# Two strided reduces in place of four pairwise maxima, and three projections moved to later rounds, in an attention and mixture-of-experts block on one core

## The chip, the core and the metric

The kernel runs on one NeuronCore of a Trainium2 chip. Its engines work from queues of their own and wait for each other by semaphores: PE (TensorE, matmuls), DVE (VectorE), ACT (ScalarE), POOL (GpSimd) and SP (SyncE, which starts transfers). The metric is the time of one execution on the device in microseconds (us). Times inside an execution come from one profiled execution and count from the start of its span.

## What is computed

A layer norm, then the input plus attention plus a mixture of experts. Attention has 4 sequences of 1024 tokens with 256 channels and one head; the mixture sends every token to 2 of 16 experts beside a shared network.

```python
xn = _layernorm(x, axis=-1)
x = x + attn(xn, Wq, bq, Wk, bk, Wv, bv) + ffn(xn, ...)

def attn(x, Wq, bq, Wk, bk, Wv, bv):
    q = jnp.einsum('bte,de->btd', x, Wq) + bq
    k = jnp.einsum('bte,de->btd', x, Wk) + bk
    v = jnp.einsum('bte,de->btd', x, Wv) + bv
    dot = jnp.einsum('bqd,bkd->bqk', q, k) / KSQRT
    p = jax.nn.softmax(dot, axis=-1)
    return jnp.einsum('bqk,bkd->bqd', p, v)
```

Everything is fp32. Each product is made of three matmuls of a high and a low part (`PASSES`), so every operand is split: ACT writes the high part, DVE the remainder.

## The kernel before

The function `plan` writes a list of steps. Every engine's program goes through the same list and does its own part of each step, in order; an engine never passes a step of its own. What sets the order of the work is thus this list alone, together with the semaphores on which a part waits.

The shared network and the experts come first, up to about 323 us. The rest, which the change touches, is attention. Its tokens are cut into 8 groups of 512 queries (`g`, 4 tiles of 128 each, tile numbers n = 4g to 4g + 3); sequence b has groups 2b and 2b + 1. The text calls the work of one g a round. A round has these steps:

- `scores` g, pair (0 to 3): PE makes the scores of 256 keys for 512 queries, 12 matmuls of 512 columns, into two banks of PSUM. `scores_copy`: ACT copies them to `scored_t` in SBUF (keys on partitions). `scored_t` is overwritten by pair 0 of the next round, so ACT waits there until the last `less` of the round before has read it.
- `scores_max`: DVE takes the maximum over the 8 key tiles for each query, elementwise, in `top_keys` (lines L1480, L1483, L1486).
- `tops`: PE turns `top_keys` (line L729, "top_keys"); `tops_max`: DVE finds each query's maximum `nmax` and spreads it to `less_wide`; `spread`: PE turns that back (L729, "less_wide").
- `less` n: DVE adds the negative maximum to the scores of tile n, giving `probs_f` (L1512, 3 buffers). `probs` n: ACT takes the exponential and copies the high part to `pT`. `probs_lo` n: DVE writes the remainder of `pT` (L1204).
- `weigh` n: PE multiplies `pT` of tile n with the values (24 matmuls, 258 columns). `weigh_sum` n: DVE divides by the sum and adds to the result `acc` (L1535, L1538), SP stores it. These four steps run in the round after, for the tiles `old` = 4(g - 1) to `old` + 3.
- `rows_in` i: DVE adds the two gathered expert rows of tile i to `acc` (L1528, twice per tile); POOL gathers the next ones (`gather`).
- projections: `heads` b, u (12 matmuls of 512 columns) makes the half u of the queries of sequence b (needed by round 2b + u) and `values` b, u (24 matmuls of 256 columns) half of its values (needed by the weighing of its tiles). ACT and DVE split the result (`heads_split`, into `qT`, L1461; `values_split`, into `vv`, L1204). These are the steps that can be moved: before the change `ahead` and `behind` name, for each round, what stands ahead of its first weigh and behind its `tops_max`.

`scores`, `heads` and `values` share two pairs of PSUM banks in turn (the "ring" in `Places`): each takes the pair that the one before the last has left, and waits until ACT and DVE have emptied it.

The lines of `scores_max` and of PE's wait for them, before:

Of the kernel before, what the change touches and what calls it, by code (L numbers as in the profile page):

```python
# [86 lines left out]
def plan():  # L87
# [119 lines left out]
    def weigh(n):  # L207
        return [("weigh", n), ("weigh_sum", n)]
# [4 lines left out]
    def probs(n):  # L213
        return [("probs", n), ("probs_lo", n)]


    ahead = {1: split("heads", 1, 1), 2: split("heads", 2, 0), 3: split("heads", 2, 1), 4: split("heads", 3, 0),
             5: split("heads", 3, 1), 6: split("values", 3, 1)}
    behind = {2: split("values", 1, 1), 3: split("values", 2, 0), 4: split("values", 2, 1), 5: split("values", 3, 0)}
    steps += [("keys_load", 1), ("ones",), *split("heads", 0, 0), *split("values", 0, 0)]  # L220
    steps += [("gather", i) for i in range(YR)]
    for g in range(GROUPS):
        new, old = CT * g, CT * (g - 1)
        steps += scores(g, 0)
        if g == 1:
            steps += probs(new - 2)
# [7 lines left out]
        if g == 0:  # L234
            steps += [*split("heads", 0, 1), ("heads", 1, 0), ("tops", g), ("tops_max", g), ("heads_split", 1, 0),
                      ("values", 0, 1), ("spread", g), ("values", 1, 0), ("less", new),
                      ("values_split", 0, 1), ("less", new + 1), ("less", new + 2), ("probs", new), ("values_split", 1, 0), ("probs", new + 1),
                      ("probs_lo", new), ("less", new + 3), ("probs_lo", new + 1), *rows(new + 2), *rows(new + 3)]
        elif g + 1 < GROUPS:
            steps += [*ahead[g], *weigh(old), ("tops", g), ("tops_max", g), *behind.get(g, []), *weigh(old + 1), ("spread", g),  # L240
                      ("less", new), ("less", new + 1), ("less", new + 2), ("probs", new), ("probs", new + 1),
                      ("probs", new + 2), ("probs_lo", new), ("less", new + 3), *weigh(old + 2), ("probs_lo", new + 1),
                      *rows(new + 2), ("probs_lo", new + 2), *rows(new + 3)]
            if g + 2 < GROUPS:
                steps += [*weigh(old + 3), *probs(new + 3)]
        else:
            steps += [("probs", new - 1), *weigh(old - 1), *weigh(old), ("tops", g), ("probs_lo", new - 1), ("tops_max", g),
                      *weigh(old + 1), ("spread", g), ("less", new), ("less", new + 1), ("less", new + 2),
                      *[("probs", new + t) for t in range(CT)], ("probs_lo", new), ("less", new + 3), *weigh(old + 2),
                      ("probs_lo", new + 1), *weigh(old + 3), ("probs_lo", new + 2), ("probs_lo", new + 3),  # L250
                      *rows(new + 2), *rows(new + 3), *sum((weigh(new + t) for t in range(CT)), [])]
# [59 lines left out]
def build(nc, x, bv, Wqkv, bqk_in, Wr, We, Ws, const_f, const_b, out):  # L311
# [4 lines left out]
    with ctx:  # L316
# [82 lines left out]
        scored_t = at("scored_t", r_h, [P, KT, CHUNK])  # L399
# [802 lines left out]
        def vector_program(e):  # L1202
# [369 lines left out]
```

## Time and profile before

| | us |
|---|---|
| median of 3 runs | 562.47 |
| lowest and highest | 562.42, 563.23 |
| the profiled execution | 562.47 |
| its span | 560.7 |
| PE busy in it | 520.9 |
| DVE busy | 396.4 |
| ACT busy | 280.4 |
| POOL busy | 191.4 |

The span is the time between the first and the last instruction; the execution's time has 1.8 us around it. Busy is the time in which an engine works on an instruction. In the timelines a row gives the start in us, the duration in us, engine, line, operation, written and read tiles, a count, and in brackets how long the engine sat idle before it and which instruction ended the wait. Where a row holds several instructions, its duration goes from the first start to the last end. Matmuls overlap: the next starts before one has ended, so their prices are read from start to start. The granted clock of TensorE has a mean of 0.991.

### The profile page before, as it was taken

How to read it: one execution, taken by the hardware profiler on the slowest of the kernel's cores; microseconds unless marked ns; L12 is line 12 of the kernel's file. 1: busy time of each engine (PE TensorE's matmuls, PEld its weight loads, DVE VectorE, ACT ScalarE, POOL GpSimd, SP SyncE). 2: the span in 40 equal slices, each digit the busy share in tenths (PEclk: the TensorE clock that was granted, in tenths of full speed). 3: DMA queues.
4: the chain of work that ended last, by engine and by line, in shares of the span. 5: the costliest groups of instructions: out<-in, count | busy, mean ns of one | idle time of the engine just before them, and what ended most of it. 6: DMA issues, size and time to landing. Idle time of an engine off the chain costs nothing.

```text
span 560.7 us, 9991 instructions
## 1 busy us (share of the span) xinstructions
PE 520.9 (93%) x3469; PEld 473.2 (84%) x3469; DVE 396.4 (71%) x806; ACT 280.4 (50%) x467; POOL 191.4 (34%) x170
## 2 busy tenths in 40 slices
PE   3999998899997899989886999999999999999997
PEld 3888987778887789988876988798989898989897
DVE  5778456998985456454453627899696969697986
ACT  3767764355643255444342544836272727272742
POOL 0001010411005666788885043244142323323410
PEclk9999999999998899999998999999999999999999
DMA  8826254302023455674447471062116111112111
GB/s 314 338 104 243 114 226 179 113 30 85 0 85 95 140 167 161 196 255 146 150 147 127 119 251 37 24 223 61 53 57 206 58 56 49 57 55 69 39 57 57
DMA packets 29888, 69.29 MB, mean 124 GB/s; under 512 B 5008, under 2 KB 9488, under 8 KB 28816
## 3 DMA queue, kind: packets, MB, share of 16 engines
q1 hardware_dynamic: 22496, 49.68, 24.7%
q0 software_dynamic: 6912, 18.88, 12.9%
q8 instruction: 30, 0.49, 0.4%
q14 instruction: 18, 0.15, 0.1%
q10 hardware_dynamic: 432, 0.09, 0.1%
HBM read 41.37 MB, written 27.26 MB: 122 GB/s over the span
## 4 chain that ended last, share of the span: by engine, by line
PE 76%; DVE 10%; another core or an unknown queue 4%; ACT 4%; issue 3%; DMA 1%; POOL 0%; SPq 0%; ACTq 0%; DVEq 0%; POOLq 0%
PE ps L723 47%; PE ps L904 8%; PE ps L729 7%; PE ps L845 6%; PE ps L925 5%; PE ps L806 1%; DVE probs_f L1512 1%; DVE blk_xT L1204 1%; ACT probs_f L1194 1%; DMA stage_gu<-in_shared 1%; ACT blk_xT L1009 1%; PE ps L815 1%; DMA blk_x<-rows,row 1%; DVE acc L1294 1%
## 5 line engine op out<-in xcount | busy, mean ns | idle before, releaser
L710 POOL DMA_INDIRECT rows_y<-ytab,slot x64 | 75.5, 1180 | 136.5 <-DVE acc L1528 120.1
L682 POOL DMA_INDIRECT blk_x<-rows,row x80 | 82.1, 1026 | 70.2 <-DVE row L1399 31.5
L723 PE MATMUL ps<-vv,pT 128*128 128x258 f32 x768 | 96.7, 284 | 0.0
L723 PE MATMUL ps<-xT,shared_w 128*128 128x512 f32 x384 | 94.3, 400 | 1.4 <-DVE sil L1280 1.4
L723 PEld LDWEIGHTS ps<-vv,pT 128*128 128x128 f32 x768 | 94.2, 189 | 0.5
L723 PEld LDWEIGHTS ps<-xT,shared_w 128*128 128x128 f32 x384 | 72.3, 192 | 16.8 <-issue 2.1
L723 PE MATMUL ps<-qT,xbT_hi 128*128 128x512 f32 x256 | 79.5, 392 | 1.0 <-ACT scored_t L1009 0.8
L904 PE MATMUL ps<-expert_w,blk_xT 128*128 x480 | 68.3, 292 | 6.6 <-DVE blk_xT L1204 6.4
L904 PEld LDWEIGHTS ps<-expert_w,blk_xT 128*128 128x128 f32 x480 | 61.1, 193 | 8.8 <-issue 8.4
L723 PEld LDWEIGHTS ps<-qT,xbT_hi 128*128 128x128 f32 x256 | 47.2, 188 | 11.9 <-ACT scored_t L1009 2.0
L668 POOL TENSOR_TENSOR expert_w<-stage_e,expert_w 128x768 fp32r<-128x768 f32 x7 | 13.6, 1941 | 115.2 <-ACT expert_w L1009 115.2
L1194 ACT ACTIVATE probs_f<-probs_f 128x1024 f32<-128x1024 f32 x32 | 33.6, 1049 | 37.7 <-DVE probs_f L1512 37.7
L723 PE MATMUL ps<-qT,xbT_lo 128*128 128x512 f32 x128 | 49.9, 390 | 0.0
L845 PE MATMUL ps<-shared_w,hT 128*128 128x256 f32 x384 | 49.6, 288 | 0.0
L1009 ACT ACTIVATE scored_t<-ps 128x1024 f32<-128x1024 f32 x32 | 32.6, 1023 | 33.0 <-PE ps L723 29.4
L845 PEld LDWEIGHTS ps<-shared_w,hT 128*128 128x128 f32 x384 | 48.1, 195 | 0.3
L1204 DVE TENSOR_TENSOR blk_xT<-ps,blk_xT 128x512 fp32r<-128x512 f32 x40 | 27.6, 689 | 25.7 <-ACT blk_xT L1009 21.0
L1132 ACT ACTIVATE blk_sil<-ps 128x256 f32<-128x256 f32 x40 | 15.4, 386 | 50.9 <-PE ps L904 24.8
L1204 DVE TENSOR_TENSOR pT<-probs_f,pT 128x1024 fp32r<-128x1024 f32 x32 | 39.0, 1219 | 2.1 <-ACT pT L1009 1.9
L925 PE MATMUL ps<-expert_w,blk_hT 128*128 x240 | 39.3, 300 | 1.1 <-DVE blk_hT L1204 1.0
L1512 DVE TENSOR_TENSOR probs_f<-scored_t,ps 128x1024 f32<-128x1024 f32 x32 | 37.6, 1215 | 1.3 <-PE ps L729 0.4
L1425 DVE TENSOR_TENSOR blk_h<-blk_sil,ps 128x256 f32<-128x256 f32 x40 | 16.7, 416 | 28.4 <-ACT blk_sil L1132 20.1
(159 smaller groups left out, 869.3 us busy)
## 6 DMA issues: line engine op xcount, KB each, us to landing
ytab<-blk_y SPq DMA_DIRECT2D x40, 256.0 KB
keys<-xT SPq DMA_DIRECT2D x8, 1024.0 KB, 5.7
stage_e<-in_experts SPq DMA_DIRECT2D x16, 384.0 KB, 3.1
rows<-xn SPq DMA_DIRECT2D x8, 512.0 KB, 2.6
xbT_hi<-keys SPq DMA_DIRECT2D x8, 512.0 KB
xbT_lo<-keys SPq DMA_DIRECT2D x8, 512.0 KB
out<-acc SPq DMA_DIRECT2D x32, 128.0 KB
acc<-in_x SPq DMA_DIRECT2D x7, 512.0 KB, 8.8
```

What stands on the lines that cost most here:

```text
L682: e.indirect_dma_start(out=blk_x[:, q, n, :], out_offset=None, in_=rows, in_offset=bass.IndirectOffsetOnAxis(ap=row[:, 2 * b + n:2 * b + n ...
L710: e.indirect_dma_start(out=rows_y[:, r, k, :], out_offset=None, in_=ytab, in_offset=bass.IndirectOffsetOnAxis(ap=slot[:, k, i:i + 1], axis=0),
L723: ins = e.matmul(dst, stationary(p, k), moving(q, k), start=(n == 0), stop=(n == total - 1))
L729: ins = e.transpose(dst[:, n * P:(n + 1) * P], s, ident)
L845: ins = e.matmul(ps[:, b, (n % 2) * D:(n % 2 + 1) * D], hT[:, p, j, n * P:(n + 1) * P], shared_w[:, q, 2 * KD * SH + j * D:2 * KD * SH + ( ...
L904: ins = e.matmul(ps[:, 2 + r, n * D:(n + 1) * D], blk_xT[:, r, p, (n * KD + k) * P:(n * KD + k + 1) * P], weights(b, n, q, k * 2 * HID, 2 ...
L925: ins = e.matmul(ps[:, 6 + r, n * D:(n + 1) * D], blk_hT[:, r, p, n * P:(n + 1) * P], weights(b, n, q, 2 * D, D), start=(at == 0), stop=(a ...
L1009: e.activation(hi, src, ACT.Copy).then_inc(done, 1)
L1194: e.activation(probs_f[w][:, :, :], probs_f[w][:, :, :], ACT.Exp).then_inc(exp_made, 1)
L1204: e.tensor_tensor(lo, src, hi.bitcast(F32), ALU.subtract).then_inc(done, 1)
L1425: e.tensor_tensor(blk_h[:, r, :, :], blk_sil[:, r, :, :], gu[:, :, HID:2 * HID], ALU.mult).then_inc(blk_hidden, 1)
L1512: e.tensor_tensor(probs_f[w][:, :, :], scored_t[:, 0:KT, t * P:(t + 1) * P], ps[:, 5, t * P:(t + 1) * P].unsqueeze(1).to_broadcast([P, KT, ...
```

## The change

It has three parts. The maximum over the 8 key tiles is made in two `tensor_reduce` on a strided view in place of three `tensor_tensor` of 1024 elements and one of 512: the first reads the first 4 tiles once the second pair of scores is copied and writes into a ninth row of `scored_t`; the second reads the last 4 tiles and that row once the fourth pair is copied. The steps ahead of and behind `tops` are made by a rule in place of the two tables, and this moves projections:

| round | projections before | after |
|---|---|---|
| 0 | heads 0.1, heads 1.0, values 0.1, values 1.0 | heads 0.1, heads 1.0, values 0.1 |
| 1 | heads 1.1 | values 1.0 |
| 2 | heads 2.0, values 1.1 | heads 1.1 |
| 3 | heads 2.1, values 2.0 | values 1.1, heads 2.0 |
| 4 | heads 3.0, values 2.1 | heads 2.1, values 2.0 |
| 5 | heads 3.1, values 3.0 | values 2.1, heads 3.0 |
| 6 | values 3.1 | heads 3.1, values 3.0, values 3.1 |

Third, `top_keys` and `less_wide` change places in SBUF, which no step waits for.

```diff
         steps += scores(g, 1)
         if g == 1:
-            steps += probs(new - 1)
-        steps += [("scores_max", g, 1), *rows(new), *scores(g, 2), ("scores_max", g, 2), *rows(new + 1)]
-        steps += [*scores(g, 3), ("scores_max", g, 3)]
-        if g in (1, 3):
-            steps.append(("keys_load", g // 2 + 2))
...
+            steps += [("probs", new - 1), ("probs_lo", new - 1)]
+        steps += [("scores_max", g, 0), *rows(new), *scores(g, 2), *rows(new + 1), *scores(g, 3), ("scores_max", g, 1)]
+        if u == 1 and b + 2 < NB:
+            steps.append(("keys_load", b + 2))
+        if first:
+            beside = [*split("heads", 0, 1), ("heads", 1, 0)], [("heads_split", 1, 0), ("values", 0, 1)], []
+            sums = [[], [], [], []]
         else:
...
+            sums = [[("weigh", old + t), ("weigh_sum", old + t)] for t in range(CT)]
+            if g == 1:
+                beside = split("values", 1, 0) + sums[0], sums[1], []
+            elif g == 2:
+                beside = split("heads", 1, 1) + sums[0], sums[1], []
+            elif u == 0:
+                beside = split("heads", b, 1) + sums[0], split("values", b, 0), sums[1]
+                if b + 1 == NB:
+                    beside[1].extend(split("values", b, 1))
+            elif not last:
+                beside = split("values", b, 1) + split("heads", b + 1, 0) + sums[0], sums[1], []
...
+        steps += [*beside[0], ("tops", g), ("tops_max", g), *beside[1], ("spread", g), *beside[2]]
+        if first:
+            steps += [("less", new), ("less", new + 1), ("less", new + 2), ("values_split", 0, 1), ("probs", new),
+                      ("probs", new + 1), ("probs_lo", new), ("less", new + 3), ("probs_lo", new + 1), *rows(new + 2), *rows(new + 3)]
...
-                    if pair == 1:
-                        if g > 0:
-                            e.wait_ge(tops_turned, g)
-                        e.tensor_tensor(top_keys[:, :, :], scored_t[:, 0:2, :], these, ALU.max).then_inc(tops_found, 1)
...
+                    g, half = a
+                    e.wait_ge(scores_copied, nth[("scores", g, 2 * half + 1)])
+                    if g > 0:
+                        e.wait_ge(tops_turned, g)
+                    if half == 1:
+                        e.wait_ge(tops_found, 2 * g + 1)
+                    these = scored_t[:, 0:KT // 2, :] if half == 0 else scored_t[:, KT // 2:KT + 1, :]
+                    e.tensor_reduce(scored_t[:, KT, :] if half == 0 else top_keys[:, :],
+                                    these.rearrange("p k q -> p q k"), X, ALU.max).then_inc(tops_found, 1)
```

What this does to the engines' queues is shown at three places. The first is DVE behind the spread turn of round 0; `qT` is the remainder of heads 1.0, `probs_f` is written by a less, the first `vv` is the remainder of values 0.1 and the second that of values 1.0. Before:

```order
L1461 SCALAR_TENSOR_TENSOR qT<-ps,mix_b,qT 128x512 x2
L1512 TENSOR_TENSOR probs_f_102<-scored_t,ps 128x1024
L1204 TENSOR_TENSOR vv<-ps,vv 128x4x256
L1512 TENSOR_TENSOR probs_f_103<-scored_t,ps 128x1024
L1512 TENSOR_TENSOR probs_f_104<-scored_t,ps 128x1024
L1204 TENSOR_TENSOR vv<-ps,vv 128x4x256
L1204 TENSOR_TENSOR pT_96<-probs_f_102,pT_96 128x1024
L1512 TENSOR_TENSOR probs_f_102<-scored_t,ps 128x1024
```

After:

```order
L1471 SCALAR_TENSOR_TENSOR qT<-ps,mix_b,qT 128x512 x2
L1516 TENSOR_TENSOR probs_f_101<-scored_t,ps 128x1024
L1516 TENSOR_TENSOR probs_f_102<-scored_t,ps 128x1024
L1516 TENSOR_TENSOR probs_f_103<-scored_t,ps 128x1024
L1214 TENSOR_TENSOR vv<-ps,vv 128x4x256
L1214 TENSOR_TENSOR pT_96<-probs_f_101,pT_96 128x1024
L1516 TENSOR_TENSOR probs_f_101<-scored_t,ps 128x1024
```

The remainder of values 0.1 went from behind one less to behind three, and that of values 1.0 is gone from here.

The second place is PE at the same point. `xbT_hi` and `xbT_lo` are the two parts of sequence 0, the names with numbers those of sequence 1; `w_v` marks a values step and `qT` scores. Before:

```order
L723 MATMUL ps<-w_v,xbT_hi 128x256 x2
L723 MATMUL ps<-w_v,xbT_lo 128x256
L729 MATMUL ps<-cf,less_wide 128x128 x4
L723 MATMUL ps<-w_v,xbT_hi_92 128x256 x2
L723 MATMUL ps<-w_v,xbT_lo_93 128x256
```

After:

```order
L733 MATMUL ps<-w_v,xbT_hi 128x256 x2
L733 MATMUL ps<-w_v,xbT_lo 128x256
L739 MATMUL ps<-cf,less_wide 128x128 x4
L733 MATMUL ps<-qT,xbT_hi 128x512 x2
L733 MATMUL ps<-qT,xbT_lo 128x512
```

Behind the spread turn came the 24 matmuls of values 1.0; now the scores of round 1 follow at once.

The third place is PE at the end of round 6, from the last matmuls of values 3.1 to the first of round 7; the matmuls with `pT` are weigh steps. Before:

```order
L723 MATMUL ps<-w_v,xbT_lo_93 128x256
L723 MATMUL ps<-vv,pT_96 128x258 x24
L729 MATMUL ps<-cf,top_keys 128x128 x4
L723 MATMUL ps<-vv,pT_97 128x258 x24
L729 MATMUL ps<-cf,less_wide 128x128 x4
L723 MATMUL ps<-vv,pT_98 128x258 x24
L723 MATMUL ps<-qT,xbT_hi_92 128x512 x2
```

After:

```order
L733 MATMUL ps<-w_v,xbT_lo_93 128x256
L739 MATMUL ps<-cf,less_wide 128x128 x4
L733 MATMUL ps<-vv,pT_97 128x258 x24
L733 MATMUL ps<-vv,pT_98 128x258 x24
L733 MATMUL ps<-qT,xbT_hi_92 128x512 x2
```

The spread turn moved ahead of the second weigh, and the first weigh with the turn of `top_keys` now stands ahead of the two values steps.

## Rows read from the trace of the kernel before

**Rows 1.** The page: the span, and PE's busy time, share, instructions.

```profile
span 560.7 us, 9991 instructions
PE 520.9 (93%) x3469; PEld 473.2 (84%) x3469; DVE 396.4 (71%) x806; ACT 280.4 (50%) x467; POOL 191.4 (34%) x170
```

**Rows 2.** Busy time by stage: stretch, length, then PE, PEld, DVE, ACT, POOL.

```profile
351.40:380.00 28.60, 27.46 (x166) 23.43 (x165) 25.92 (x34) 17.11 (x19) 9.53 (x8) 1.00 0.36 121
380.00:408.90 28.90, 28.90 (x190) 26.55 (x189) 23.29 (x35) 14.44 (x16) 9.46 (x8) 1.00 0.18 55
...
518.90:560.70 41.80, 38.55 (x275) 35.84 (x273) 33.13 (x53) 19.01 (x19) 7.92 (x6) 1.00 0.17 51
```

**Rows 3.** Timeline of PE, round 2 and the first matmuls of round 3.

```profile
380.00 0.63 PE L723 MATMUL ps<-qT,xbT_hi 128*128 128x512 f32 x2
...
390.90 0.39 PE L723 MATMUL ps<-xbT_hi,w_mix 128*128 128x512 f32 x1
...
393.62 3.06 PE L723 MATMUL ps<-vv,pT 128*128 128x258 f32 x24
...
396.88 0.48 PE L723 MATMUL ps<-w_v,xbT_hi 128*128 128x256 f32 x2
...
399.83 3.05 PE L723 MATMUL ps<-vv,pT 128*128 128x258 f32 x24
...
403.07 6.02 PE L723 MATMUL ps<-vv,pT 128*128 128x258 f32 x48
408.93 0.63 PE L723 MATMUL ps<-qT,xbT_hi 128*128 128x512 f32 x2
```

**Rows 4.** Timeline of PE, end of round 0 and round 1.

```profile
348.44 0.48 PE L723 MATMUL ps<-w_v,xbT_hi 128*128 128x256 f32 x2
...
354.52 0.73 PE L723 MATMUL ps<-qT,xbT_hi 128*128 128x512 f32 x2 [0.22 <-DVE vv L1204]
...
358.09 0.73 PE L723 MATMUL ps<-qT,xbT_hi 128*128 128x512 f32 x2 [0.54 <-ACT scored_t L1009]
...
364.00 0.50 PE L723 MATMUL ps<-xbT_hi,w_mix 128*128 128x512 f32 x1
...
370.30 0.66 PE L729 MATMUL ps<-cf,top_keys 128*128 128x128 f32 x4 [0.39 <-DVE top_keys L1486]
```

**Rows 5.** Timeline of DVE, entry of round 1, and the last maximum of round 3.

```profile
348.72 1.22 DVE L1512 TENSOR_TENSOR probs_f<-scored_t,ps 128x1024 f32<-128x1024 f32 x1 [0.37 <-PE ps L729]
...
353.25 1.22 DVE L1204 TENSOR_TENSOR vv<-ps,vv 128x1024 fp32r<-128x1024 f32 x1
...
355.70 1.22 DVE L1512 TENSOR_TENSOR probs_f<-scored_t,ps 128x1024 f32<-128x1024 f32 x1
...
364.20 1.22 DVE L1480 TENSOR_TENSOR top_keys<-scored_t 128x1024 f32<-128x1024 f32 x1
365.34 1.00 DVE L1528 SCALAR_TENSOR_TENSOR acc<-rows_y,score,acc 128x256 f32<-128x256 f32 x2
...
421.08 1.23 DVE L1483 TENSOR_TENSOR top_keys<-top_keys,scored_t 128x1024 f32<-128x1024 f32 x1 [0.58 <-ACT scored_t L1009]
```

**Rows 6.** Timeline of ACT: the first scores copy of rounds 1 and 3.

```profile
357.01 1.02 ACT L1009 ACTIVATE scored_t<-ps 128x1024 f32<-128x1024 f32 x1 [1.94 <-DVE probs_f L1512]
...
412.94 1.01 ACT L1009 ACTIVATE scored_t<-ps 128x1024 f32<-128x1024 f32 x1
```

**Rows 7.** Groups of DVE by line and form: count, busy us, mean ns, idle before.

```profile
L1483 DVE TENSOR_TENSOR top_keys<-top_keys,scored_t 128x1024 f32<-128x1024 f32 x15 | 18.3, 1222 | 5.6 <-ACT scored_t L1009 4.2 <-issue 1.3
...
L1486 DVE TENSOR_TENSOR top_keys<-top_keys 128x512 f32<-128x512 f32 x8 | 5.5, 692 | 0.3
...
L1407 DVE TENSOR_REDUCE blk_f<-blk_tmp 128x80 f32<-128x1280 f32 x1 | 1.5, 1479 | 0.0
```

**Rows 8.** Timeline of PE: the third scores step of round 7.

```profile
524.90 0.73 PE L723 MATMUL ps<-qT,xbT_hi 128*128 128x512 f32 x2 [0.26 <-ACT scored_t L1009]
```

**Rows 9.** Groups of DVE: two operations that read with a step of 32 bytes.

```profile
L1304 DVE CAST ek<-idx 128x32 f32<-128x32 uint32 x2 | 0.3, 178 | 0.0
...
L1305 DVE TENSOR_TENSOR gap<-top 128x32 f32<-128x32 f32 x1 | 0.2, 208 | 0.0
```

More of the change, by code:

```diff
@@ L207, in weigh @@
     def weigh(n):
-        return [("weigh", n), ("weigh_sum", n)]
+        return [("weigh", n)]
     def rows(i):
         return [("rows_in", i), *([("gather", i + YR)] if i + YR < TILES else [])]
[L213 to L219, printed above, removed]
     steps += [("keys_load", 1), ("ones",), *split("heads", 0, 0), *split("values", 0, 0)]
@@ L222, in plan @@
     for g in range(GROUPS):
+        b, u = divmod(g, 2)
         new, old = CT * g, CT * (g - 1)
+        first, last = g == 0, g == GROUPS - 1
         steps += scores(g, 0)
         if g == 1:
-            steps += probs(new - 2)
+            steps += [("probs", new - 2), ("probs_lo", new - 2)]
         steps += scores(g, 1)
         if g == 1:
-            steps += probs(new - 1)
-        steps += [("scores_max", g, 1), *rows(new), *scores(g, 2), ("scores_max", g, 2), *rows(new + 1)]
-        steps += [*scores(g, 3), ("scores_max", g, 3)]
@@ L232, in plan @@
-        if g in (1, 3):
-            steps.append(("keys_load", g // 2 + 2))
[L234 to L245, printed above, removed]
-        else:
[L247 to L251, printed above, removed]
@@ new lines, in plan @@
+        if last:
+            steps += [("probs", new - 1), ("weigh", old - 1), ("weigh_sum", old - 1), *sums[0], ("tops", g), ("probs_lo", new - 1), ("tops_max", g), *sums[1], ("spread", g),
+                      ("less", new), ("less", new + 1), ("less", new + 2), *[("probs", new + t) for t in range(CT)],
+                      ("probs_lo", new), ("less", new + 3), *sums[2], ("probs_lo", new + 1), *sums[3], ("probs_lo", new + 2),
+                      ("probs_lo", new + 3), *rows(new + 2), *rows(new + 3)]
+            continue
@@ new lines, in plan @@
+        steps += [*beside[0], ("tops", g), ("tops_max", g), *beside[1], ("spread", g), *beside[2]]
+        if first:
+            steps += [("less", new), ("less", new + 1), ("less", new + 2), ("values_split", 0, 1), ("probs", new),
+                      ("probs", new + 1), ("probs_lo", new), ("less", new + 3), ("probs_lo", new + 1), *rows(new + 2), *rows(new + 3)]
+            continue
+        steps += [("less", new), ("less", new + 1), ("less", new + 2), ("probs", new), ("probs", new + 1), ("probs", new + 2),
+                  ("probs_lo", new), ("less", new + 3), *sums[2], ("probs_lo", new + 1), *rows(new + 2), ("probs_lo", new + 2),
+                  *rows(new + 3)]
@@ L252, in plan @@
+        if g + 2 < GROUPS:
+            steps += [*sums[3], ("probs", new + 3), ("probs_lo", new + 3)]
+    for n in range(TILES - CT, TILES):
+        steps += [("weigh", n), ("weigh_sum", n)]
     return steps
@@ L397, in build @@
               at(f"pT{CT - 1}", r_xr, [P, 2, NT], F32R)]
-        scored_t = at("scored_t", r_h, [P, KT, CHUNK])
-        top_keys = at("top_keys", r_h + 4 * KT * CHUNK, [P, 2, CHUNK])
-        r_late = r_h + 4 * (KT + 2) * CHUNK
+        scored_t = at("scored_t", r_h, [P, KT + 1, CHUNK])
+        r_late = r_h + 4 * (KT + 1) * CHUNK
         probs_f = [at("probs_f0", r_pT + 3 * PART, [P, KT, P]), at("probs_f1", r_late, [P, KT, P]),
                    at("probs_f2", r_xn + 4 * YR * 2 * D, [P, KT, P])]
-        less_wide = at("less_wide", r_pT + 3 * PART + 4 * NT, [P, CT, P])
+        top_keys = at("top_keys", r_pT + 3 * PART + 4 * NT, [P, CHUNK])
+        less_wide = at("less_wide", r_late + 4 * NT, [P, CT, P])
         rows_y = at("rows_y", r_xn, [P, YR, 2, D])
@@ L972, in tensor_program @@
                     g = a[0]
[L973 removed]
+                    e.wait_ge(tops_found, 2 * (g + 1))
                     if g == 0:
@@ L977, in tensor_program @@
                         e.wait_ge(less_made, 3 * g - 2)
-                    turn(ps[:, 4, :], [top_keys[:, 0, t * P:(t + 1) * P] for t in range(CT)], tops_turned)
+                    turn(ps[:, 4, :], [top_keys[:, t * P:(t + 1) * P] for t in range(CT)], tops_turned)
                 elif kind == "spread":
```

12 lines of the change are left out of this document (removed).

## The prediction, made before the changed kernel had run

> **Names.** A round is one g of the plan (0 to 7). "Scores" are its four steps of 12 matmuls of 512 columns; "projection" means a heads step (12 of 512) or a values step (24 of 256). The remainder of a heads step is written to qT, that of a values step to vv, both by DVE.
>
> **What bounds the kernel now.** I read first the page's busy line [rows 1]: PE is busy for 520.9 of 560.7 us. The plan is the same up to round 0, so only the stretch from 328 us on can change. I cut that at the starts of the rounds and read each engine's busy time [rows 2]: round 2 (380.0 to 408.9) has PE busy for all of its 28.90 us and DVE for 23.29; round 1 (351.4 to 380.0) has PE idle for 28.60 - 27.46 = 1.14; from the start of round 7 to the end it is busy for 38.55 of 41.80, and 2.9 of the difference is the tail behind the last matmul. So PE sets the time of this stretch, and what can be won is small. The timeline of PE in round 2 [rows 3] gives the prices on PE, from start to start: scores 390.90 - 380.00 = 10.90, heads 393.62 - 390.90 = 2.72, values 399.83 - 396.88 = 2.95 at most (24 x 120 ns = 2.88), one weigh (408.93 - 403.07)/2 = 2.93, and of the round's 408.93 - 380.00 = 28.93 the rest, 28.93 - 10.90 - 2.72 - 2.88 - 4 x 2.93 = 0.71, is two turns of four tiles, 0.36 each. Nothing is left for a wait. Idle time stands in two places only: at the entry of round 1 [rows 4], where scores 1.1 begins at 354.52, scores 1.2 at 358.09 and the turn of top_keys at 370.30 after a wait, and in round 7, where the third scores step waits 0.26 us [rows 8].
>
> **Part 1: the order. Round 0 and 1.** The whole work of PE is the same before and after. Before, rounds 0 to 7 hold 4, 1, 2, 2, 2, 2, 1, 0 projections; afterwards 3, 1, 1, 2, 2, 2, 3, 0. Values 1.0 leaves round 0 for round 1, and heads 1.1 leaves round 1 for round 2. So at the end of round 1 PE has 2.72 us less behind it (heads 1.1), and the question is by how much round 1 ends earlier.
>
> Before, values 1.0 (2.9 us from 348.44 [rows 4]) covers the time in which DVE makes the first probabilities. Its cover is gone: scores 1.0 begins at 348.44 and ends at 351.16. Scores 1.1 then needs the pair of banks that values 0.1 filled (the ring alternates), so it waits for the remainder vv of values 0.1. On DVE this was second in line, behind one less; now it is fourth, behind three. The first less began at 348.72, three take to 352.1 (from there to 353.25 four instructions of this size started, 1.13 us each [rows 5]), and vv ends at 353.4. Scores 1.1 begins at 353.4, after a wait of 2.3 us from 351.16, and ends at 356.1.
>
> Scores 1.2 waits for ACT's copy of scores 1.0, and this for the fourth less, as scored_t is overwritten. Before: less at 355.70 [rows 5], copy at 357.01 [rows 6], scores 1.2 at 358.09. Ahead of that less, DVE now has one vv remainder less (values 1.0's), worth 1.13 us of its queue. So everything from there is early by 1.1: copy at 355.9, scores 1.2 at 357.0, and the projection behind the scores at 362.9 in place of 364.0. This entry is a chain of DVE and ACT, not of PE: taking 2.9 us of PE's work out of it returns 1.1.
>
> **Part 2: the maximum.** Per round three tensor_tensor of 1024 elements and one of 512 become two reduces, over 4 x 512 and over 5 x 512 inputs. Before: 3 x 1.22 + 0.69 = 4.36 us [rows 7]. The trace has a reduce over 1280 contiguous inputs in SBUF: 1479 ns [rows 7], that is 1280/0.96 + 0.146. By that row the two cost 2048/0.96 ns + 0.15 = 2.28 and 2560/0.96 ns + 0.15 = 2.81, together 5.1: 0.75 us more on DVE per round, of which most lies behind the last scores copy (2.81 against 1.22 + 0.69).
>
> What hides it: in a full round, the last maximum begins 12.15 us after the round (421.08 - 408.93 [rows 3, 5]) and would end at 14.9 or 15.0; PE turns top_keys at 10.90 + 2.72 + 2.93 = 16.55 or later. Slack 1.6, no cost. In rounds 3 and 5 weigh needs the values split of this round, which ends 1.2 later at 16.1 against 16.5: still covered, by 0.4. In round 7 the turn comes after two weighs: covered. In round 1 it is not, as DVE is late there: before, the first maximum began at 364.20 [rows 5] and PE waited 0.39 for top_keys. Now it begins at 363.1, ends at 365.3, four additions of rows follow (two of them 1.00 [rows 5], less an overlap of 0.09), the second goes from 367.1 to 369.9. The turn begins at 370.0, PE having been free from 362.9 + 2.9 + 2.9 = 368.7. Before: 370.30. At this point the kernel is 0.3 us early with 2.72 us of work outstanding: **+2.4 us**.
>
> What is a price with two ends is the strided read: the new reduces step 2048 bytes from one input to the next, and no row does this. The nearest are two small ones with a step of 32 bytes [rows 9]: the cast of 32 indices took 178 ns, less than 32/0.96 + 157 = 190, so no penalty; the difference of 32 top values, with two such inputs, took 208 against about 190 (0.16 fixed, by the 692 ns of 512 elements [rows 7]), so 0.55 ns more per element, about 1.5 times. The reduces have one input stream, as the cast has, so I take no penalty and keep 1.5 times as the other end.
>
> In the sum above nothing hangs on a page. The Trainium skill, in SBUF — State Buffer (Door 1: The DMA port swizzle), says that SBUF is read in lines of 16 bytes, that two hits on a line are needed for the full rate, and that fp32 can thus be strided only up to 4 elements for free. It gives no factor; it speaks against this change, and the cast's row does not agree with it.
>
> **Part 3: rounds 2 to 6.** Round 2 with heads 1.1 alone costs PE 28.93 - 2.88 = 26.05; DVE's 23.29 [rows 2] lose a vv of 1.1 and gain 0.75, so some 22.9. Rounds with two projections come to 24.0 of 28.93. PE stays the bound, nothing is lost or won. In round 4 and 6 the spread turn is now ahead of the second weigh. DVE still does that weigh's sum ahead of the first less, so the less stays tied to the weigh's end, while PE has 0.36 us less to do before it needs ACT's copy of the next scores. That slack was 414.38 (408.93 + 5.45) less 413.95 (412.94 + 1.01 [rows 6]), 0.4: round 4 loses nothing, or 0.1. Round 7 already waited there [rows 8]: it waits **0.36 us** longer. The 5.6 us of projections that went to round 6 thus meet no idle time that they could fill. The tail behind it is unchanged.
>
> **Sum.** +2.4 + 0.36 = +2.8 us. The profiled execution's span of 560.7 becomes 563.5; its time is 562.47, also the median, 1.8 above the span. So 565.2 us, +0.5%; this case alone spans 564.0 to 566.4 (two links of the entry chain and the hand-offs, about 0.1 us each, and a slack of 0.4 us in rounds 3, 4 and 5 that may be missed).
>
> **Rivals.**
> 1. The strided reduces take 1.5 times as long per input: 3.4 and 4.2 us, 2.5 more per round. Round 0 then loses 1.0 (values 0.1 waits for qT's remainder), round 1 another 2.5, rounds 3 and 5 1.05 each (weigh waits for vv, whose 0.4 of slack is gone), rounds 2, 4 and 7 together 1.0. Sum 6.5: 571.7 us. For it speaks the row of 208 ns, against it the cast's.
> 2. The strided read goes at half rate, 4.4 and 5.5 us. This is worked from rows alone, with every input taking 2.08 ns: +3.0 in round 0, +4.9 in round 1, +3.3 in rounds 3 and 5 each, about +2.3 in 2, 4, 6 and 7 each, 23.7 more: 589 us. The cast at 178 ns would have taken 223, which speaks against it. It is what the skill's rule of the line would do, taken as one access in two.
> 3. Faster: the 2.72 us of postponed projection costs nothing, because round 6 or 7 would have stood idle for it, and the 1.1 us of the shorter DVE queue at the entry is kept. 562.47 - 1.1 = 561.4. It decides once more than 1.6 us of PE's time between 380 us and its last matmul is idle. The trace shows 0.4 [rows 2], and round 2 with none; only time hidden inside the modelled ends of matmuls could hold it.
> 4. Same: the wait before scores 1.1 is overlapped better than I have it (vv's remainder handed over earlier) and round 7 loses nothing: 562.5 to 563.5.
>
> **How the numbers follow.** The forecast has 0.72, rival 1 0.12, rival 2 0.05, rival 3 0.05, rival 4 0.06. A measurement can tell 0.2% (1.1 us) from no change. Slower is forecast and rivals 1 and 2, 0.89; same 0.06; faster 0.05. The range goes from 562.8, inside rival 4, to 571.7, which takes in rival 1 and leaves out 2 and 3 and a part of 4.
>
> **What would show it.** PE: idle of about 2.2 us before scores 1.1 with DVE's vv remainder as releaser, and about 1.2 before the turn of top_keys in round 1; 2.72 more in rounds 2 to 7 with no new waits but 0.3 in round 7. DVE: reduces of 2.28 and 2.81 us. If they show over 3 us, rival 1 or 2 holds. ACT: the first scores copy of round 1 about 1.1 us earlier. Wrong would be: no wait before scores 1.1, or PE waits in rounds 2 to 6.

## The result, and the profile after

The changed kernel is slower: 581.08 us (median of 4 runs, 580.26 to 581.31) against 562.44 us (561.40 to 563.23), a ratio of 1.033 with a 95% interval of 1.031 to 1.035. The profiled execution took 582.04 us, with a span of 580.2. The prediction was 565.2 us in a range of 562.8 to 571.7: the direction was right, the size was not, and the time lies outside the range.

The page of the changed kernel, beside [rows 1]: PE's busy time rose by 7 us and DVE's by 32.

```profile
span 580.2 us, 9967 instructions
PE 527.9 (91%) x3469; PEld 478.1 (82%) x3469; DVE 428.4 (74%) x790; ACT 280.6 (48%) x467; POOL 182.0 (31%) x170
```

The groups of DVE from 325 us on, by line and form (count, busy us, mean ns, idle before), beside [rows 7]: the two new reduces take 4697 and 3830 ns. The prediction had 2810 and 2280.

```profile
L1490 DVE TENSOR_REDUCE top_keys<-scored_t 128x512 f32<-128x2560 f32 x8 | 37.6, 4697 | 0.0
L1490 DVE TENSOR_REDUCE scored_t<-scored_t 128x512 f32<-128x2048 f32 x8 | 30.6, 3830 | 4.3 <-issue 4.3
```

With some 150 ns of fixed time taken off (the prediction's figure), that is (4697 - 150)/2560 = 1.78 ns and (3830 - 150)/2048 = 1.80 ns per input, against (1479 - 150)/1280 = 1.04 ns in the contiguous reduce of [rows 7].

What PE waited for in the same stretch (in total, times, longest):

```profile
PE ps L739 <- DVE top_keys L1490: 7.4, 6, 4.0
PE ps L733 <- issue: 3.7, 2, 2.0
PE ps L733 <- DVE vv L1214: 2.0, 1, 2.0
...
```

Two more waits of 0.7 us each follow, one for DVE's remainder qT in round 0 and one for ACT's copy of scores in round 7; the sum is 14.5 us, where the same stretch held 1.4 before.

And where these waits stand, in the timeline of PE:

```profile
350.73 0.60 PE L739 MATMUL ps<-cf,less_wide 128*128 128x128 f32 x4
356.03 0.73 PE L733 MATMUL ps<-qT,xbT_hi 128*128 128x512 f32 x2 [1.96 <-DVE vv L1214]
...
375.88 1.11 PE L739 MATMUL ps<-cf,top_keys 128*128 128x128 f32 x4 [4.04 <-DVE top_keys L1490]
376.65 5.18 PE L733 MATMUL ps<-vv,pT 128*128 128x258 f32 x24
381.67 0.60 PE L739 MATMUL ps<-cf,less_wide 128*128 128x128 f32 x4
382.02 6.02 PE L733 MATMUL ps<-vv,pT 128*128 128x258 f32 x48
...
408.99 6.02 PE L733 MATMUL ps<-vv,pT 128*128 128x258 f32 x48
...
433.25 3.11 PE L733 MATMUL ps<-vv,pT 128*128 128x258 f32 x24 [1.73 <-issue]
...
439.87 6.03 PE L733 MATMUL ps<-vv,pT 128*128 128x258 f32 x48
...
466.84 8.87 PE L733 MATMUL ps<-vv,pT 128*128 128x258 f32 x72
...
494.44 3.15 PE L733 MATMUL ps<-vv,pT 128*128 128x258 f32 x24 [1.99 <-issue]
...
501.12 6.02 PE L733 MATMUL ps<-vv,pT 128*128 128x258 f32 x48
...
530.84 6.04 PE L733 MATMUL ps<-vv,pT 128*128 128x258 f32 x48
543.08 0.73 PE L733 MATMUL ps<-qT,xbT_hi 128*128 128x512 f32 x2 [0.71 <-ACT scored_t L1019]
...
559.87 17.51 PE L733 MATMUL ps<-vv,pT 128*128 128x258 f32 x144
```

The two waits marked "issue" stand ahead of the first weigh of rounds 3 and 5. The first weigh is where the order makes PE wait for the vv remainder of the values step just made, and DVE's timeline fits: in round 3 that remainder (431.94, 1.20 us) starts when the second reduce ends, and weigh begins at 433.25. That DVE is what PE waits for there is read from this order of times; the profile itself names no releaser.

A round begins where its two or three last weighs end (5.86 us for two, 8.78 for three, after their start). The spans of the two profiled executions differ by 580.2 - 560.7 = 19.5 us. Of that 1.0 us lies ahead of the rounds, which the change does not touch (round 0 begins at 328.38 before and at 329.37 after). The rest comes apart as follows, each round against what its work costs PE by the prediction's prices:

| stretch | before or expected, us | measured, us | more |
|---|---|---|---|
| round 0, up to the spread turn | 19.70 | 350.73 - 329.37 = 21.36 | 1.66 |
| round 1 (from there to round 2; 2.72 us of work left out) | 31.92 - 2.72 | 387.88 - 350.73 = 37.15 | 7.95 |
| round 2 | 26.05 | 26.97 | 0.92 |
| round 3 | 28.93 | 30.88 | 1.95 |
| round 4 | 28.93 | 29.89 | 0.96 |
| round 5 | 28.93 | 31.36 | 2.43 |
| round 6 | 28.88 | 29.72 | 0.84 |
| round 7, to the last matmul | 38.88 | 577.38 - 536.70 = 40.68 | 1.80 |
| sum | | | 18.5 |

Round 1 holds a second loss. Busy time by stage (stretch, length, PE busy, granted clock, DMA share, GB/s) shows the clock, in the last two rows for the weigh behind the wait of 4.04 us and for what follows:

```profile
351.10:368.80 17.70, 15.74 (x75) 0.90 0.16 43
368.80:376.60 7.80, 3.76 (x30) 0.86 0.82 293
376.60:381.70 5.10, 5.10 (x27) 0.54 0.16 51
381.70:387.90 6.20, 6.20 (x55) 1.00 0.08 25
```

The clock was at 0.50 until 381.0, the lower of the two levels (1.2 of 2.4 GHz), and then back at 1.00, which makes the mean of 0.54. That weigh took 381.67 - 376.65 = 5.02 us where it takes 2.93 otherwise, and the turn ahead of it 0.77 where it takes 0.41: 2.4 us that no wait shows.

The first row has a second drop: read in halves of a microsecond, the clock is at 0.50 from about 357.4 to 360.7 too, in scores 1.1 and 1.2, behind the wait of 1.96 us. PE lost some 1.6 us there (from 356.03 to 361.17 for matmuls that take 3.5 at the full clock). As far as the trace shows it cost nothing: ACT, which copies these scores, worked without a gap from 358.53 to 365.45, and PE, had it been faster, would have waited for DVE by as much more than 4.04 us.

Of the 18.5 us, 14.5 - 1.4 = 13.1 are thus more waiting, 2.4 the clock behind the long wait and some 1.6 the clock ahead of it; 1.4 are not assigned.

### The profile page after: what moved, and what is told of

Read it like the earlier page. It is cut to its first block, busy times and chain, and to the rows that moved or that the text cites. A ratio compares the mean times of both kernels' runs of the same rounds, so it can differ in the third digit from the quotient of the medians.

```text
span 580.2 us, 9967 instructions
## 1 busy us (share of the span) xinstructions
PE 527.9 (91%) x3469; PEld 478.1 (82%) x3469; DVE 428.4 (74%) x790; ACT 280.6 (48%) x467; POOL 182.0 (31%) x170
## 4 chain that ended last, share of the span: by engine, by line
PE 60%; DVE 23%; issue 8%; ACT 3%; another core or an unknown queue 3%; DMA 1%; POOL 0%; SPq 0%; DVEq 0%; ACTq 0%; POOLq 0%
PE ps L733 30%; PE ps L914 9%; PE ps L739 7%; PE ps L855 7%; PE ps L935 5%; DVE top_keys L1490 4%; DVE scored_t L1490 3%; DVE pT L1214 3%; DVE probs_f L1516 3%; DVE acc L1532 2%; PE ps L816 1%; DVE acc L1304 1%; DMA stage_gu<-in_shared 1%; DVE blk_xT L1214 1%
## 5 line engine op out<-in xcount | busy, mean ns | idle before, releaser
L720 POOL DMA_INDIRECT rows_y<-ytab,slot x64 | 66.8, 1044 | 162.3 <-DVE acc L1532 146.0
L733 PE MATMUL ps<-vv,pT 128*128 128x258 f32 x768 | 98.6, 288 | 3.7 <-issue 3.7
L733 PEld LDWEIGHTS ps<-vv,pT 128*128 128x128 f32 x768 | 95.9, 193 | 5.1 <-issue 4.7
```

The source lines that it names most:

```text
L720: e.indirect_dma_start(out=rows_y[:, r, k, :], out_offset=None, in_=ytab, in_offset=bass.IndirectOffsetOnAxis(ap=slot[:, k, i:i + 1], axis=0),
L733: ins = e.matmul(dst, stationary(p, k), moving(q, k), start=(n == 0), stop=(n == total - 1))
```

## The experiments

They ran on three other chips, where the kernel before takes 551 to 552 us. The difference lies ahead of attention: the spread turn of round 0, at 348.08 before, stands at 337 to 340 in these traces, and rounds that the edit does not touch are as long (rounds 2 and 3 of the last experiment 28.93 each, against 28.93 and 28.89). So ratios are compared, each against the kernel before on the same chip. As a second measure stands, for some, the time from the start of that turn to the end of the last matmul, which is 557.81 - 348.08 = 209.73 us before.

### The order alone, the maximum alone

```diff
-        steps += [("scores_max", g, 0), *rows(new), *scores(g, 2), *rows(new + 1), *scores(g, 3), ("scores_max", g, 1)]
+        steps += [("scores_max", g, 1), *rows(new), *scores(g, 2), ("scores_max", g, 2), *rows(new + 1)]
+        steps += [*scores(g, 3), ("scores_max", g, 3)]
```

This is the new order with the old maxima (their code and the tiles' places as in the kernel before).

> The changed order of the steps with the four pairwise maxima of the kernel before (3 x 1.22 + 0.69 us). Theory (the strided reduces make nearly all of the loss): only the entry of round 1 and the wait in round 7 cost: 562.4 + 1.7 + 0.4 = 564.5 us, with about 2 us of PE idle before scores 1.1. Rival (the order, by the lost cover, makes most of it): 575 us or more. If the order is free: 562.4.

Measured: 1.0040 (1.0026 to 1.0055), 553.16 against 550.95 us, and 212.0 us for the second measure, 2.3 more. The theory holds: the order costs 2.2 us, and the rival's 575 is far off. The entry of round 1, in the timeline of PE:

```profile
337.14 0.60 PE L739 MATMUL ps<-cf,less_wide 128*128 128x128 f32 x4
342.45 0.72 PE L733 MATMUL ps<-qT,xbT_hi 128*128 128x512 f32 x2 [1.96 <-DVE vv L1214]
...
358.24 0.66 PE L739 MATMUL ps<-cf,top_keys 128*128 128x128 f32 x4 [0.29 <-DVE top_keys L1496]
```

From the spread turn to that of top_keys it is 21.10 us, 1.12 less than the 370.30 - 348.08 = 22.22 before, with 2.72 us of work left out: 1.6 lost there, as expected, and the wait in round 7 is 0.70 where it was 0.26.

The other half takes the changed kernel and gives it the steps of the kernel before, with the two reduces:

```diff
+    ahead = {1: split("heads", 1, 1), 2: split("heads", 2, 0), 3: split("heads", 2, 1), 4: split("heads", 3, 0),
+             5: split("heads", 3, 1), 6: split("values", 3, 1)}
+    behind = {2: split("values", 1, 1), 3: split("values", 2, 0), 4: split("values", 2, 1), 5: split("values", 3, 0)}
...
+        steps += [("scores_max", g, 0), *rows(new), *scores(g, 2), *rows(new + 1)]
+        steps += [*scores(g, 3), ("scores_max", g, 1)]
```

> The order of the kernel before with the two strided reduces (3.83 and 4.70 us in the changed kernel). Theory: PE waits for top_keys in every round: 1.5 in round 0, about 4 and some 2 for a lower clock behind it in round 1, about 1 in each of rounds 2 to 6, 1.8 in round 7: 577 us. Rival (order): 566 us or less.

Measured: 1.0255 (1.0239 to 1.0271), 565.26 us. On the scale of the kernel before that is 562.44 x 1.0255 = 576.8, as expected. PE waits for top_keys in all eight rounds:

```profile
PE ps L730 <- DVE top_keys L1481: 8.9, 8, 4.4
```

The two halves give 14.1 + 2.2 = 16.3 us, the whole 3.3% of 551, some 18.2, so 1.9 are left over. By the second measure it is 11.4 + 2.3 against 16.9, so 3.2. The waits say what makes it: the new order puts a values step ahead of the first weigh in rounds 3 and 5, and the long reduce delays its remainder (1.73 and 1.99 us of wait, where this half pays 0.64 and 0.59 for top_keys instead). Neither half alone has that wait. The clock fell in this half too: behind the wait of 4.40 us in round 1 the weigh took 371.07 - 366.41 = 4.66 us at a granted clock of 0.59.

### The step between inputs

```diff
-                                    these.rearrange("p k q -> p q k"), X, ALU.max).then_inc(tops_found, 1)
+                                    these.rearrange("p k q -> p (k q)").rearrange("p (q k) -> p q k", q=CHUNK), X, ALU.max).then_inc(tops_found, 1)
```

> The changed kernel, but both reduces read the same number of inputs with a step of 4 bytes instead of 2048 (four or five neighbours are reduced, so what they compute is another maximum; all counts and waits stay). Theory (it is the step that makes the reduces slow): 2.28 and 2.81 us each, and 565.2 us as the prediction's sum had it. Rival (a reduce is slow here whatever its step, by its length or the other engines' traffic): 3.8 and 4.7 us and 581 us.

Measured: 1.0071 (1.0056 to 1.0085), 555.16 us, and the reduces, by line and form:

```profile
L1490 DVE TENSOR_REDUCE top_keys<-scored_t 128x512 f32<-128x2560 f32 x8 | 22.6, 2819 | 7.4 <-ACT scored_t L1019 7.4
L1490 DVE TENSOR_REDUCE scored_t<-scored_t 128x512 f32<-128x2048 f32 x8 | 18.2, 2279 | 4.3 <-ACT scored_t L1019 4.3
```

2279 and 2819 ns are the prediction's 2.28 and 2.81. The same counts, the same traffic around them and another step: it is the step. This kernel is also the one that the prediction's sum describes: PE waits 1.95 us before scores 1.1, 1.09 before the turn of top_keys in round 1 and 0.71 in round 7, where 2.2, 1.2 and 0.6 were forecast. The second measure is 212.82, 3.1 us more than before, for a forecast of 2.8: 2.3 of it in round 1 and 0.4 in round 7, for 2.4 and 0.36.

### How a step becomes slow

To measure the price by itself, DVE was given extra work behind its last result, when no other engine works. Both kernels of this kind were executed once; what is read from them is the length of single instructions. For example:

```python
for s in (1, 2, 3, 4, 8):      # step of 4 s bytes
    v = probe[:, 0:2048 * s].rearrange("p (q k s) -> p q k s", k=4, s=s)[:, :, :, 0]
    next_probe(e.tensor_reduce(probe_out[:, 0:512], v, X, ALU.max))
```

> The kernel before with extra work of DVE behind its last result, where no other engine works: reduces of 2048 inputs to 512 with steps of 4, 8, 12, 16, 32 bytes between inputs, then with 16, 64, 256, 512 bytes inside a transposed view, then over 2, 4, 5, 8 tiles with a step of 2048 bytes, then copies and two-input maxima with steps of 4, 8, 16 and 32 bytes. Theory by lines (any input on a new line of 16 bytes is slow): 2.28 us up to 12 bytes, 3.8 from 16 on. Rival by distance (only steps of hundreds of bytes are slow, as the cast with 32 bytes took 178 ns): 2.28 up to 64 bytes, 3.8 at 512 and 2048. If both are wrong and it is contention with other engines: 2.28 everywhere here.

The timeline of DVE, in the order of the expectation; the first five are reduces of 2048 inputs, four per output, with 4, 8, 12, 16 and 32 bytes between them:

```profile
564.63 2.29 DVE L1557 TENSOR_REDUCE probe_out<-probe 128x512 f32<-128x2048 f32 x1
566.96 2.29 DVE L1557 TENSOR_REDUCE probe_out<-probe 128x512 f32<-128x2048 f32 x1
569.28 2.85 DVE L1557 TENSOR_REDUCE probe_out<-probe 128x512 f32<-128x2048 f32 x1
572.16 3.74 DVE L1557 TENSOR_REDUCE probe_out<-probe 128x512 f32<-128x2048 f32 x1
575.93 3.81 DVE L1557 TENSOR_REDUCE probe_out<-probe 128x512 f32<-128x2048 f32 x1
...
594.50 1.23 DVE L1563 TENSOR_REDUCE probe_out<-probe 128x512 f32<-128x1024 f32 x1
595.76 3.62 DVE L1563 TENSOR_REDUCE probe_out<-probe 128x512 f32<-128x2048 f32 x1
...
612.25 1.23 DVE L1566 COPY probe_out<-probe 128x2048 f32<-128x2048 f32 x1
...
615.53 2.00 DVE L1566 COPY probe_out<-probe 128x2048 f32<-128x2048 f32 x1
...
618.83 1.23 DVE L1570 TENSOR_TENSOR probe_out<-probe 128x1024 f32<-128x1024 f32 x1
620.09 1.96 DVE L1570 TENSOR_TENSOR probe_out<-probe 128x1024 f32<-128x1024 f32 x1
```

The theory by lines is right as to the step, but for 12 bytes, where it had 2.28 us and 2.85 was measured: from 16 bytes on a reduce over four takes 3.6 to 3.8 us (3.62 at 256 and 512 bytes), and other engines have no part in it. Copies (8 and 32 bytes here) go from 1.23 to 2.00 us and two-input maxima (8 and 16 bytes) from 1.23 to 1.96. But one row did not fit: the reduce over two tiles with 2048 bytes (at 594.50) is not slow at all. Nor was a reduce over three tiles in the kernel (the shorter second reduce, below); so a second set of probes asked about the number of inputs in turn.

> The kernel before with extra reduces of DVE behind its last result, over 2, 3 and 4 inputs per output: with 16, 64 and 2048 bytes between the inputs, then over 3, 4 and 5 with 2080 bytes, then copies that read 2, 3 and 4 tiles in turn with 2048 bytes. Theory (what is slow is to read more than three lines of 16 bytes in turn, whatever their distance, since a reduce over 3 rows took 1.15 ns per input and one over 4 and 5 took 1.78): 2 and 3 in turn near 1.04 to 1.15 ns per input at every distance, 4 and 5 at 1.7 to 1.8. Rival (only rows 2048 bytes apart share something, so the distance counts): 4 inputs at 2080 bytes or at 64 bytes are fast.

```profile
564.29 1.24 DVE L1559 TENSOR_REDUCE probe_out<-probe 128x512 f32<-128x1024 f32 x1
565.56 1.88 DVE L1559 TENSOR_REDUCE probe_out<-probe 128x512 f32<-128x1536 f32 x1
567.47 3.78 DVE L1559 TENSOR_REDUCE probe_out<-probe 128x512 f32<-128x2048 f32 x1
...
578.08 1.23 DVE L1559 TENSOR_REDUCE probe_out<-probe 128x512 f32<-128x1024 f32 x1
579.34 1.91 DVE L1559 TENSOR_REDUCE probe_out<-probe 128x512 f32<-128x1536 f32 x1
581.29 3.62 DVE L1559 TENSOR_REDUCE probe_out<-probe 128x512 f32<-128x2048 f32 x1
584.94 1.91 DVE L1562 TENSOR_REDUCE probe_out<-probe 128x512 f32<-128x1536 f32 x1
586.89 3.62 DVE L1562 TENSOR_REDUCE probe_out<-probe 128x512 f32<-128x2048 f32 x1
...
596.00 1.04 DVE L1565 COPY probe_out<-probe 128x1536 f32<-128x1536 f32 x1
597.07 2.00 DVE L1565 COPY probe_out<-probe 128x2048 f32<-128x2048 f32 x1
```

Over two, three and four inputs it is 1.24, 1.88 and 3.78 us with 16 bytes between them, and 1.23, 1.91 and 3.62 with 2048 (64 bytes gave 1.24, 1.88 and 3.57); with 2080 bytes three and four take 1.91 and 3.62. At these distances it is the number in turn that counts: a view that comes back to the same 16 bytes after one or two others runs at 1.05 to 1.15 ns per input, one that visits four or more in turn at 1.7 to 1.8. That it is the order of the reads, and not the number of inputs that a reduce folds into one output, the copies show, which fold nothing: reading two, three and four tiles in turn they take 0.70, 1.04 and 2.00 us for 1024, 1536 and 2048 elements, so 0.53, 0.57 and 0.90 ns each. Why the limit lies between three and four was not looked into.

The Trainium skill's rule (SBUF — State Buffer, Door 1: The DMA port swizzle: lines of 16 bytes, two hits on a line for the full rate, a penalty for each access to a new line) agrees with the plain steps: full rate at 4 and 8 bytes, slow from 16 on. It does not agree with the views over two or three tiles, which change the line with every input and take 1.24 and 1.88 us; there the measurement decides.

### A shorter second reduce

```diff
-                    these = scored_t[:, 0:KT // 2, :] if half == 0 else scored_t[:, KT // 2:KT + 1, :]
+                    these = scored_t[:, 0:KT // 2, :] if half == 0 else scored_t[:, KT // 2 + 2:KT + 1, :]
```

> The changed kernel, but the second reduce reads three rows of 512 instead of five (it leaves the key tiles 4 and 5 out of the maximum). By the rate of the first (1.78 us per 1000 inputs) it takes 2.9 us instead of 4.7, still with a step of 2048 bytes. Theory (only the time behind the last scores copy costs, beyond a slack of 1.6 us): the waits for top_keys fall to 0 in rounds 0, 2, 4, 6 and 7 and to about 2.2 in round 1, weigh waits for vv in rounds 3 and 5 nearly vanish; about 8 us over the order alone and 2 of them back by the clock: 1.011 to 1.015 times the kernel before. Rival (DVE's total is what counts, 6.8 us per round still being over the 4.4 of before): over 1.022.

Measured: 1.0070 (1.0050 to 1.0089), and the second reduce took 1916 ns, not 2900: three rows in turn are not slow, which was not known when this was expected. The size in the expectation was thus wrong, and the loss is below both figures. What the run does decide: DVE spends 3.83 + 1.92 = 5.75 us per round on the maximum, 1.4 more than before and 0.65 more than with the unit step, and the loss is the same 0.7%. The first reduce alone, slow as it is, costs nothing but in round 1 (wait of 1.79 us for top_keys); DVE's total is not what counts, what stands behind the last copy of scores is. That part is as long here (1.92 us) as with the old maxima (1.22 + 0.69), and the second measure is 213.47, 1.5 us above the order alone, as much as the two waits in round 1 differ (1.79 and 0.29).

### The clock behind the long wait

```diff
             if g == 1:
-                beside = split("values", 1, 0) + sums[0], sums[1], []
+                beside = split("values", 1, 0) + split("heads", 1, 1) + sums[0], sums[1], []
             elif g == 2:
-                beside = split("heads", 1, 1) + sums[0], sums[1], []
+                beside = sums[0], sums[1], []
```

> The changed kernel with heads 1.1 in round 1, behind values 1.0, and no projection in round 2. PE's idle time before the turn of top_keys moves: 4.0 to about 1.3 in round 1, 0.6 to about 3.3 in round 2, same sum. Theory (the clock at half speed in the weigh behind the wait of 4 us in round 1 costs 2.1 us, and came from that wait): that weigh takes 2.9 us in place of 5.0; the whole is 1.029 times the kernel before in place of 1.033, unless the wait of 3.3 in round 2 lowers the clock there. Rival (the low clock has to do with the place, with the transfers of keys in round 1 for instance, and not with the wait): 5.0 us again and 1.033.

Measured: 1.0371 (1.0356 to 1.0387), not faster than the changed kernel with its 1.033. By the second measure the two are almost the same, 226.94 against 226.65 us; the rest of the 0.4% lies ahead of it and was not traced. The timeline of PE shows why nothing was gained:

```profile
365.16 0.66 PE L739 MATMUL ps<-cf,top_keys 128*128 128x128 f32 x4 [1.47 <-DVE top_keys L1490]
365.57 3.15 PE L733 MATMUL ps<-vv,pT 128*128 128x258 f32 x24
369.72 0.66 PE L739 MATMUL ps<-cf,less_wide 128*128 128x128 f32 x4 [1.00 <-DVE less_wide L1508]
...
392.99 0.66 PE L739 MATMUL ps<-cf,top_keys 128*128 128x128 f32 x4 [3.04 <-DVE top_keys L1490]
393.40 4.66 PE L733 MATMUL ps<-vv,pT 128*128 128x258 f32 x24
```

The waits moved as expected, 1.47 and 3.04 us, and the low clock moved with the long one: the weigh of round 1 runs at full speed (granted clock 1.00), that of round 2, behind 3.04 us of idle PE, takes 4.50 us (granted clock 0.62). So this drop follows the long wait and not the place, and the rival is out. The length of one wait is not all that counts, though: in scores 1.1, behind a wait of 1.96 us, the clock was at 0.50 here (346 to 349 us) as in the changed kernel, and at 1.00 behind the same wait with the order alone, the unit step and the shorter second reduce. The two that fell had also waited 0.53 and 0.66 us in round 0, the three others had not; whether that decides was not tried. Of the gain in round 1, 1.6 us were given back in round 2, and a new wait of 1.0 came on top, as DVE had two remainders to write between the reduce and less_wide.

### The cover of values 1.0

The order of the changed kernel with the old maxima, as in the first experiment, but round 0 keeps values 1.0 and round 1 heads 1.1:

```diff
-            beside = [*split("heads", 0, 1), ("heads", 1, 0)], [("heads_split", 1, 0), ("values", 0, 1)], []
+            beside = ([*split("heads", 0, 1), ("heads", 1, 0)],
+                      [("heads_split", 1, 0), ("values", 0, 1)], [("values", 1, 0)])
...
             if g == 1:
-                beside = split("values", 1, 0) + sums[0], sums[1], []
+                beside = split("heads", 1, 1) + sums[0], sums[1], []
             elif g == 2:
-                beside = split("heads", 1, 1) + sums[0], sums[1], []
+                beside = sums[0], sums[1], []
```

> The order of the changed kernel with the pairwise maxima, but values 1.0 stays in round 0 and heads 1.1 in round 1, with DVE's order of the kernel before there; the other moves stand (round 2 has no projection, round 6 three). Theory (of the order's 2.2 us the entry of round 1 makes 1.7 to 1.9, the longer wait in round 7 the rest): no wait of 2 us before scores 1.1, 0.7 in round 7, 1.0007 times the kernel before. Rival (the fuller round 6 or the emptier round 2 costs): 1.003 or more.

Measured: 1.0023 (1.0012 to 1.0034), between the two; the interval leaves out the theory's 1.0007 and not the rival's 1.003. The wait of 2 us before scores 1.1 is gone, and from the spread turn of round 0 to the turn of top_keys it is 22.23 us, against 22.22 before, with nothing left out: the 1.6 us of the entry belong to the lost cover. But 1.2 us remain in the second measure, not 0.4. By the starts of the rounds 0.4 of it is in round 2, where without any projection PE comes to the turn before top_keys is there, 0.4 in round 7 (wait of 0.71), and the rest, 0.3, in rounds 3 to 6, most of it in round 5. A round without any projection is thus not free, even with the old maxima.

### Another entry for round 1

The kernel before, with this in its plan:

```diff
-        steps += scores(g, 0)
-        if g == 1:
-            steps += probs(new - 2)
-        steps += scores(g, 1)
-        if g == 1:
-            steps += probs(new - 1)
-        steps += [("scores_max", g, 1), *rows(new), *scores(g, 2), ("scores_max", g, 2), *rows(new + 1)]
-        steps += [*scores(g, 3), ("scores_max", g, 3)]
+        steps += [*scores(g, 0), *scores(g, 1)]
+        if g == 1:
+            steps.append(("probs", new - 2))
+        steps += [("scores_max", g, 1), *rows(new), *scores(g, 2)]
+        if g == 1:
+            steps += [("probs_lo", new - 2), ("probs", new - 1)]
+        steps += [("scores_max", g, 2), *rows(new + 1)]
+        if g == 1:
+            steps.append(("probs_lo", new - 1))
+        steps += [*scores(g, 3), ("scores_max", g, 3)]
```

> The kernel before with another order at the entry of round 1 alone: ACT copies the second scores before it makes the probabilities of tile 2, and makes those of tile 3 behind the third scores copy; DVE writes the remainders of both tiles later by as much. Theory (that entry is a chain of ACT and DVE, by which PE waits): scores 1.3 and the turn of top_keys begin earlier, by 0.2 and about 1.1 us: 0.998. Rival (the chain moves elsewhere, to the probabilities): 1.000 or slower.

Measured: 0.9987 (0.9978 to 0.9996), 551.02 against 551.72 us, and 208.63 for the second measure, 1.1 less. The turn of top_keys comes 359.03 - 337.81 = 21.22 us after the spread turn, 1.0 earlier than before, and no wait stands before it:

```profile
337.81 0.60 PE L731 MATMUL ps<-cf,less_wide 128*128 128x128 f32 x4
...
359.03 0.60 PE L731 MATMUL ps<-cf,top_keys 128*128 128x128 f32 x4
```

This version is the fastest of all, if by little: it takes part of the idle time at that entry, the largest that the kernel before has behind 328 us.

## Why the prediction was right or wrong

**What bounds the kernel.** Right: PE sets the time of this stretch, and of the 18.5 us lost 13.1 show as waits of PE and some 4.0 as its clock (1.6 of them would otherwise have been waiting).

**Part 1, the order.** Right in its mechanism and nearly in size. It gave a wait of 2.3 us before scores 1.1 (1.96 measured), an entry earlier by 1.1 (1.12 in the order alone) and 2.72 us of work left over. The order by itself costs 2.2 us.

**Part 2, the maximum.** Here is the step that failed: "The reduces have one input stream, as the cast has, so I take no penalty". With it the step's price was put at nothing; measured, it is 3.83 and 4.70 us in place of 2.28 and 2.81, 3.4 us more per round. The cast of 178 ns [rows 9] was held against 1.04 ns per element, 190 ns. But a copy of fp32 in SBUF takes 0.52 ns per element when its inputs lie side by side (2048 in 1.23 us) and 0.90 ns when they lie 32 bytes apart (2.00 us). If the cast runs as the copy does, 32 elements make 157 + 17 = 174 ns unhindered and 157 + 29 = 186 slowed, and 178 lies between them: the row could not tell, and a slowed one would still have looked fast against 190. Nor is one input stream an exemption, as both reduce and copy are slowed. The other row, 208 ns with two inputs, was the true one: the probe with 32 bytes gives 1.99 us for 1024 pairs, 1.80 ns each, or 215 ns for 32. The prediction kept it only as the other end, and as 1.5 times in place of 1.7.

The rest of that part held. With a unit step the reduces took 2279 and 2819 ns, and the kernel 1.0071 times the one before, 566.4 us on its scale, against 565.2.

**Part 3.** Near for round 7 (0.36 us more; 0.26 became 0.71), and right that the projections in round 6 fill nothing. By the table of the change ten projections stand one round later, and not three as the title counts; the sum goes by the number in each round, which is right. The slack of 0.4 us ahead of weigh in rounds 3 and 5 was seen, and rival 1 has it gone at 1.05 us each; with the longer reduces these rounds lost 1.95 and 2.43.

**The rivals.** Rival 1 (1.59 ns per input, 571.7 us) and rival 2 (2.08 ns, 589 us) had the mechanism, with 0.17 of chance together. The measured 1.78 ns lies between them: 571.7 + (0.19/0.49) x 17.3 = 578.4, an estimate made afterwards. With the 2.4 us of the clock behind the wait of 4.04 us in round 1, which no part of the prediction priced, it is 580.8, for 581.08 measured; that it comes so near is in part luck, as both ends were rough sums. Rival 2 is what one access in two would have been, and the chip is better than that. Rivals 3 and 4 are out: no wait was absorbed. The range was too narrow, since its upper end rested on a factor read from one small row.

**What would show it.** The text said that reduces over 3 us would mean rival 1 or 2, and so the profile answered at once.

## What to carry to other kernels

A row that is to price a strided read must be compared with the same operation on neighbouring inputs, and be long enough to tell; a copy can go from 0.52 to 0.90 ns per element and still stay below the 1.04 ns of a reduce. Replacing elementwise maxima by a reduce across tiles gained nothing on DVE at any number tried: three tiles of 512 take 1.91 us in one reduce and would take 2 x 0.69 us as two maxima (an estimate from [rows 7]), and from four tiles in turn on each input costs 1.7 times as much. The last operation behind the last input should stay the short one. A step that seems movable may be the cover of a chain on other engines: taking 2.9 us of matmuls out of such an entry returned 1.1.

## What the runs showed of the hardware

- A DVE read of fp32 in SBUF that goes on by 16 bytes or more with every input costs 1.7 to 1.8 ns per input in a reduce over four, five or eight, 1.8 ns per pair in a two-input maximum and 0.9 ns per element in a copy; with 4 or 8 bytes it is 1.04, 1.04 and 0.5. With 12 bytes a reduce over four is between, 2.85 us for 2048. The second input of the maximum was stepped like the first; one alone was not tried.
- A view that reads two or three places in turn and comes back to each escapes it, at all distances tried (16, 64 and 2048 bytes, for three also 2080): 1.05 and 1.15 ns per input in a reduce, 0.53 and 0.57 per element in a copy (2048 bytes only).
- PE stood idle for 4.40, 4.04 and 3.04 us in three runs, and the weigh behind it ran at a granted clock of 0.59, 0.54 and 0.62 (4.66, 5.02 and 4.50 us in place of 2.93); behind waits of 1.79 and 1.47 us it ran at 1.00. Behind a wait of 1.96 us before scores 1.1 the clock fell to 0.50 for some 3 us in the two runs that had also waited 0.53 and 0.66 us in round 0, and stayed at 1.00 in the three that had not.
